# A mixture-of-experts loop in 64-row matmul pairs, with a ring of four results that GpSimd copies

## What is computed

```python
ggates, gidx = _topk_gates(xf @ Wg + bg, 2)                  # 2 of 4 groups
egates, eidx = _topk_gates(einsum('nd,gde->nge', xf, We) + be, 4)   # 4 of 8 experts in each
combine = gw[:, :, None] * ew                                # weight of each token and expert
for g in range(4):
    h = gelu(einsum('nd,edm->enm', xf, W1[g]) + b1[g][:, None, :])  # 192 -> 768
    o = einsum('enm,emd->end', h, W2[g]) + b2[g][:, None, :]        # 768 -> 192
    y = y + einsum('end,ne->nd', o, combine[:, g, :])
```

## Time and profile before

| | us |
|---|---|
| median of three runs | 752.56 |
| the three runs | 750.7, 752.56, 757.16 |
| the profiled execution | 756.36 |
| its span, first to last instruction | 754.6 |
| TensorE busy in the span | 679.0 |
| GpSimd busy in the span | 304.8 |
| VectorE busy in the span | 406.5 |
| ScalarE busy in the span | 239.0 |

### The profile page before, as it was taken

How to read it: one execution, slowest core, us unless ns; L and a number is a source line. 1 busy time by engine, 2 the same in 40 slices (tenths; PEclk the granted TensorE clock), 3 DMA queues, 4 the chain that set the end, 5 groups by cost and what they waited for, 6 DMA issues and landing times.

```text
span 754.6 us, 20437 instructions
## 1 busy us (share of the span) xinstructions
PE 679.0 (90%) x6550; PEld 574.3 (76%) x6550; DVE 406.5 (54%) x1222; ACT 239.0 (32%) x686; POOL 304.8 (40%) x288
## 2 busy tenths in 40 slices
PE   6986948898989999876899799999999999999994
PEld 4754735655755797753799699999999999999994
DVE  6645572845489688878544234444444444444442
ACT  3322312123238311115143233333333333333331
POOL 0111820011023636302354455555655555656554
PEclk9996959587999999975699899999999999999998
DMA  9910000000000003041258454465546566565422
GB/s 325 266 41 2 2 3 2 3 1 3 1 1 0 2 1 120 8 162 50 52 151 234 113 140 127 121 171 113 129 106 178 147 172 171 117 173 126 97 46 39
DMA packets 36136, 70.07 MB, mean 93 GB/s; under 512 B 6481, under 2 KB 21362, under 8 KB 36082
## 3 DMA queue, kind: packets, MB, share of 16 engines
q0 software_dynamic: 15840, 17.71, 13.9%
q10 hardware_dynamic: 8064, 33.12, 12.8%
q1 hardware_dynamic: 12178, 18.48, 7.9%
HBM read 59.31 MB, written 9.98 MB: 92 GB/s over the span
## 4 chain that ended last, share of the span: by engine, by line
PE 72%; DVE 17%; issue 4%; DMA 3%; ACT 1%; POOL 1%; DVEq 0%; ACTq 0%; POOLq 0%; SPq 0%
PE bank L1617 20%; PE bank L1609 14%; PE bank L1612 9%; PE bank L1435 4%; PE bank L1589 4%; PE bank L1367 4%; PE bank L1299 3%; DMA out_dram<-arena,number_u 2%; PE bank L1387 2%; DVE stats L941 1%; DVE zx L955 1%; PE bank L1378 1%; DVE arena L1175 1%; DVE arena L1172 1%; PE bank L1405 1%
## 5 line engine op out<-in xcount | busy, mean ns | idle before, releaser
L654 POOL DMA_INDIRECT out_dram<-arena,number_u x80 | 126.8, 1585 | 54.9 <-DMA out_dram<-arena,number_u 28.1
L648 POOL DMA_INDIRECT arena<-normed_rows,fetch_u x80 | 78.4, 980 | 113.8 <-DMA out_dram<-arena,number_u 42.1
L841 ACT ACTIVATE arena<-bank,arena 128x128 f32<-128x128 f32 x234 | 64.6, 375 | 120.9 <-PE bank L1612 116.9
L1260 DVE COPY arena<-bank 128x256 f32<-128x256 f32 x81 | 34.4, 425 | 118.4 <-PE bank L1589 109.8
L1617 PE MATMUL bank<-arena 128*128 128x192 f32 x468 | 83.4, 327 | 0.7 <-ACT arena L841 0.7
L1617 PEld LDWEIGHTS bank<-arena 128*128 128x128 f32 x468 | 76.0, 191 | 1.0 <-ACT arena L841 1.0
L1279 DVE TENSOR_SCALAR arena<-bank,arena 128x192 f32 x80 | 33.4, 418 | 62.2 <-PE bank L1617 60.6
L1609 PE MATMUL bank<-arena 128*128 128x128 f32 x468 | 60.1, 279 | 4.3 <-DVE arena L1260 4.3
L1609 PEld LDWEIGHTS bank<-arena 128*128 128x128 f32 x468 | 58.3, 195 | 5.1 <-DVE arena L1260 5.1
L551 POOL TENSOR_SCALAR rstd<-mv 128x4 f32<-128x4 f32 (+1 forms) x15 | 3.6, 237 | 143.5 <-DVE mv L944 143.5
L841 ACT ACTIVATE arena<-bank,w_space 128x128 f32<-128x128 f32 x132 | 36.4, 375 | 68.6 <-PE bank L1612 68.6
(11 more groups left out here) (259 smaller groups left out, 1235.0 us busy)
## 6 DMA issues: line engine op xcount, KB each, us to landing
arena<-in_moe_w_dram ACTq DMA_DIRECT2D x14, 579.0 KB, 5.7
arena<-in_moe_w_dram ACTq DMA_DIRECT2D x14, 576.0 KB, 4.3
arena<-in_xf_dram SPq DMA_DIRECT2D x16, 256.0 KB, 10.6
w_space<-in_moe_w_dram ACTq DMA_DIRECT2D x7, 579.0 KB, 5.4
w2small<-in_moe_w_dram ACTq DMA_DIRECT2D x7, 579.0 KB, 5.7
w_space<-in_moe_w_dram ACTq DMA_DIRECT2D x7, 576.0 KB, 3.8
wab<-in_moe_w_dram ACTq DMA_DIRECT2D x7, 576.0 KB, 4.1
arena<-in_w_dram SPq DMA_DIRECT2D x8, 480.0 KB, 7.4
```

The source lines that it names most:

```text
L648: pool.indirect_dma_start(out=mo_stage[:, s * ROWN:(s + 1) * ROWN], out_offset=None, in_=normed_rows, in_offset=bass.IndirectOffsetOnAxis( ...
L654: pool.indirect_dma_start(out=out, out_offset=bass.IndirectOffsetOnAxis(ap=number_u[:, s:s + 1], axis=0), in_=mo_res[:, s * D:(s + 1) * D] ...
L841: nc.scalar.activation(mo_hT[:, m, :], bank[2 + m][:, 0:P], ACT.Gelu, bias=b1[:, m:m + 1]).then_inc(free[2 + m], 1)
L1260: nc.vector.tensor_copy(mo_xT.rearrange("p k t -> p (k t)"), bank[1][:, 0:2 * P]).then_inc(free[1], 1)
```

## The change

Both layers and the transposes run on 64 rows. The weights of the first layer are laid out so that each half of the partitions holds three of the six chunks; the rows of a tile are staged twice, once for each half, and their transposes come out in both halves of the array, behind the first layer's results in banks 2 and 5. A tile makes 9 pairs for the first layer, 3 pairs of transposes and 6 pairs for the second layer, whose halves go to banks 0 and 1 and are added by VectorE. TensorE waits for the rows to transpose ahead of the last pair of the first layer. VectorE writes its scaled result into a ring of four; GpSimd copies it from there to `mo_res`, copies the row numbers too, and waits for its copy before the store. VectorE's 32 experts are written out, with the bounds loaded one expert ahead.

```diff
+CHUNKS = D // 64
+HIDDEN_DONE = tuple(m + half for m in range(MC // 2) for half in (0, MC // 2))
+COLUMNS_AT, COLUMN_BANKS = P, (2, 2 + MC // 2)
+RESULTS = 4
-W1N = HID + MC // 2 * P
+W1N = MC // 2 * CHUNKS * P
...
-                use(5, "table", 1)
+                use(7, "table", 1)
...
+            pool.sem_inc(sem("result_free"), RESULTS)
             with pool.Fori(0, pairs) as pair:
...
+                    tile, new = pool.snap(i + 0), pool.snap(i % RESULTS * D)
                     pool.wait_ge(sem(f"accumulated{s}"), added)
-                    pool.sem_inc(sem("result_free"), 1)
+                    nc.gpsimd.tensor_copy(number_u[:, s:s + 1], table_u[:, bass.ds(tile, 1)])
                     pool.wait_ge(sem("fetch_set"), fetch_set)
...
                     pool.wait_ge(sem("result_ready"), result)
+                    pool.sem_inc(sem("adding"), 1)
+                    nc.gpsimd.tensor_copy(mo_res[:, s * D:(s + 1) * D], mo_new[:, bass.ds(new, D)]).then_inc(sem("result_free"), 1)
+                    pool.wait_ge(sem("result_free"), pool.snap(i + (RESULTS + 1)))
                     pool.sem_inc(sem("adding"), 1)
                     pool.wait_ge(sem(f"accumulated{1 - s}"), settled)
...
-                    act.wait_ge(full[0], i + moe_base[0])
-                    for m in range(MC):
+                    act.wait_ge(full[1], i + moe_base[1])
+                    for m in HIDDEN_DONE:
...
             def stage_rows(i):
                 dve.wait_ge(sem("rows_in"), i * 16 + 16)
-                dve.wait_ge(full[1], i + moe_base[1])
+                if not isinstance(i, int) or i:
+                    dve.wait_ge(sem("columns_full"), i)
                 nc.vector.tensor_copy(mo_gates[:, bass.ds(i % 4 * NE, NE)], mo_stage[:, bass.ds(i % STAGE * ROWN + D, NE)])
-                nc.vector.tensor_copy(mo_x[:, D:2 * P], mo_stage[:, bass.ds(i % STAGE * ROWN + P, REST)])
-                nc.vector.tensor_copy(mo_x[:, 0:D], mo_stage[:, bass.ds(i % STAGE * ROWN, D)]).then_inc(sem("rows_staged"), 1)
+                for half in range(2):
+                    ins = nc.vector.tensor_copy(mo_x.rearrange("p (k h x) -> p k h x", k=CHUNKS, h=2)[:, :, half, :], mo_stage[:, bass.ds(i % STAGE * ROWN, D)].rearrange("p (k x) -> p k x", k=CHUNKS))
+                ins.then_inc(sem("rows_staged"), 1)
 
             def take_columns(i):
-                dve.wait_ge(full[1], i + (moe_base[1] + 1))
-                nc.vector.tensor_copy(mo_xT.rearrange("p k t -> p (k t)"), bank[1][:, 0:2 * P]).then_inc(free[1], 1)
+                dve.wait_ge(sem("columns_full"), i + 1)
+                for r, b in zip((0, REST), COLUMN_BANKS):
+                    ins = nc.vector.tensor_copy(mo_xT[:, :, r:r + REST], bank[b][:, COLUMNS_AT:COLUMNS_AT + D].rearrange("p (k t) -> p k t", k=CHUNKS))
+                ins.then_inc(sem("columns_taken"), 1)
...
-                    dve.wait_ge(full[0], summing)
-                    ts(out=mo_new[:, bass.ds(new, D)], in0=bank[0][:, 0:D], scalar1=mo_gates[:, bass.ds(gate, 1)], scalar2=None, op0=ALU.mult).then_inc(free[0], 1)
-                    dve.sem_inc(sem("scaling"), 1)
                     dve.wait_ge(sem("result_free"), added)
                     dve.sem_inc(sem("scaling"), 1)
-                    nc.vector.tensor_copy(number_u[:, bass.ds(half, 1)], table_u[:, bass.ds(tile, 1)])
-                    dve.wait_ge(free[0], summing)
-                    nc.vector.tensor_copy(mo_res[:, bass.ds(to, D)], mo_new[:, bass.ds(new, D)]).then_inc(sem("result_ready"), 1)
+                    dve.wait_ge(full[0], low)
+                    ts(out=mo_new[:, bass.ds(new, D)], in0=bank[0][:, 0:D], scalar1=mo_gates[:, bass.ds(gate, 1)], scalar2=None, op0=ALU.mult).then_inc(free[0], 1)
+                    dve.wait_ge(full[1], high)
+                    dve.wait_ge(free[0], low)
+                    stt(out=mo_new[:, bass.ds(new, D)], in0=bank[1][:, 0:D], scalar=mo_gates[:, bass.ds(gate, 1)], in1=mo_new[:, bass.ds(new, D)], op0=ALU.mult, op1=ALU.add).then_inc(free[1], 1)
+                    dve.wait_ge(free[1], high)
+                    dve.sem_inc(sem("result_ready"), 1)
+
+            first, end = expert_start(dve, 0, 0), expert_start(dve, 1, 1)
+            for e in range(NE):
+                after = expert_start(dve, e + 2, 1) if e + 2 <= NE else None
+                weighted_tiles(e, first, end)
+                first, end = end, after
...
+            def transpose_rows():
+                for k in range(CHUNKS):
+                    at = COLUMNS_AT + k * REST
+                    for r, b in zip((0, REST), COLUMN_BANKS):
+                        ins = nc.tensor.transpose(bank[b][:, at:at + REST], mo_x[r:r + REST, k * P:(k + 1) * P], ident[r:r + REST, r:r + REST])
+                ins.then_inc(sem("columns_full"), 1)
...
-                    pe.wait_ge(free[1], i + (moe_base[1] + 1))
-                    for m in range(MC):
-                        mm(bank[2 + m][:, 0:P], w1e[:, m * P:(m + 1) * P], mo_xT[:, 0, :], start=True, stop=False)
-                    for m in range(MC):
-                        r, c = m % 2 * REST, HID + m // 2 * P
-                        mm(bank[2 + m][:, 0:P], w1e[r:r + REST, c:c + P], mo_xT[r:r + REST, 1, :], start=False, stop=True).then_inc(full[2 + m], 1)
-                    transpose_rows(i + 1)
+                    pe.wait_ge(sem("columns_taken"), i + 1)
+                    for n in range(MC // 2):
+                        for k in range(CHUNKS):
+                            c = (n * CHUNKS + k) * P
+                            if n * CHUNKS + k == MC // 2 * CHUNKS - 1:
+                                pe.wait_ge(sem("rows_staged"), i + 2)
+                                for b in COLUMN_BANKS:
+                                    pe.wait_ge(free[b], i + (moe_base[b] + 1))
+                            for r, m in ((0, n), (REST, n + MC // 2)):
+                                ins = mm(bank[2 + m][:, 0:P], w1e[r:r + REST, c:c + P], mo_xT[r:r + REST, k, :], start=(k == 0), stop=(k == CHUNKS - 1))
+                                if k == CHUNKS - 1:
+                                    ins.then_inc(full[2 + m], 1)
+                    transpose_rows()
                     pe.wait_ge(free[0], i + moe_base[0])
-                    for m in range(MC):
+                    pe.wait_ge(free[1], i + moe_base[1])
+                    for n, m in enumerate(HIDDEN_DONE):
                         pe.wait_ge(free[2 + m], i + (moe_base[2 + m] + 1))
-                        ins = mm(bank[0][:, 0:D], mo_hT[:, m, :], w2e[:, m, :], start=(m == 0), stop=(m == MC - 1))
-                    ins.then_inc(full[0], 1)
+                        for r, b in ((0, 0), (REST, 1)):
+                            ins = mm(bank[b][:, 0:D], mo_hT[r:r + REST, m, :], w2e[r:r + REST, m, :], start=(n == 0), stop=(n == MC - 1))
+                            if n == MC - 1:
+                                ins.then_inc(full[b], 1)
```

More of the change, by code:

```diff
@@ L291, in vit_tower @@
         mo_gates = view(P, 4 * NE)
-        mo_x = view(P, 2 * P)
-        mo_xT = view(P, 2 * P).rearrange("p (k t) -> p k t", k=2)
+        mo_x = view(P, CHUNKS * P)
+        mo_xT = view(P, CHUNKS * P).rearrange("p (k t) -> p k t", k=CHUNKS)
         mo_res = view(P, 2 * D)
-        mo_new = view(P, 4 * D)
+        mo_new = view(P, RESULTS * D)
         mo_w1 = [w1_space[:, 0:W1N], wab[:, 0:W1N]] + [view(P, W1N) for _ in range(2)]
@@ L831, in expert @@
                 if e and e + AHEAD - 1 < NE:
-                    act.wait_ge(full[0], first + moe_base[0])
+                    act.wait_ge(full[1], first + moe_base[1])
                     load_expert(act, (u + AHEAD - 1) % AHEAD, e + AHEAD - 1)
@@ L1266, in _, with weighted_tiles @@
             stage_rows(1)
-            with dve.Fori(0, NE) as e:
-                first = dve.value_load(starts[0:1, bass.ds(e, 1)], min_val=0, max_val=MAXT - 1)
-                end = dve.value_load(starts[0:1, bass.ds(e + 1, 1)], min_val=1, max_val=MAXT)
+            def weighted_tiles(e, first, end):
                 with dve.Fori(first, end) as i:
@@ L1272, in _ @@
                     stage_rows(i + 2)
-                    gate, to = dve.snap(i % 4 * NE + e), dve.snap(i % 2 * D)
-                    new = dve.snap(i % 4 * D)
-                    added, summing = dve.snap(i + 1), dve.snap(i + (moe_base[0] + 1))
-                    half, tile, ahead = dve.snap(i % 2), dve.snap(i + 0), dve.snap(i + 4)
+                    gate, new = dve.snap(i % 4 * NE + e), dve.snap(i % RESULTS * D)
+                    added, low, high = dve.snap(i + 1), dve.snap(i + (moe_base[0] + 1)), dve.snap(i + (moe_base[1] + 1))
+                    half, ahead = dve.snap(i % 2), dve.snap(i + 4)
                     nc.vector.tensor_copy(fetch_u[:, bass.ds(half, 1)], table_u[:, bass.ds(ahead, 1)]).then_inc(sem("fetch_set"), 1)
-                    dve.wait_ge(full[0], summing)
```

(20 more changed lines are left out.)

3 lines of the change are left out of this document (1 added, 2 removed).

## The result

The changed kernel takes 779.39 us in the median (776.01 to 788.1), the kernel before 752.11: a ratio of 1.0345, with a 95% interval from 1.0288 to 1.0401. One of its four runs, that of 788.1 us, was in a slower state and is left out of the ratio; the median of the other three is 777.07. The profiled execution took 776.01 us, its span 774.2; that is 19.7 more than the profiled execution of before, and the loop holds nearly all of it.

The account below looks back on a forecast made before the run. TensorE sets the pace at 4.53 us a tile, with GpSimd as late. GpSimd's loop grows 28.5 us to 395.3, less half of 5: +26 on the profiled 756.36 gives 782, less 3.8 to the median, 778; range 738 to 798.

Parts of the forecast that it names:

- the mechanism that it named: GpSimd's loop: two added copies and a wait lengthen undisturbed fetch spacing, so late landings are not made up; +26 us.
- The distance: GpSimd's loop: undisturbed time from one fetch start to the next grows from 3.50 to 4.37 us.
- The long distances: GpSimd's loop: 28 fetch spacings stretched by landings late behind expert loads, together 172.4 us, were to stay.
- The step to the median: Whole run: 3.8 us subtracted from 782, as the profiled execution before lay that far above its median; 778.
- TensorE's tile: TensorE, one tile of 128 rows: 4.53 us becomes 4.35, 0.18 saved, 14 us in all.
- The wait ahead of the last first-layer pair: TensorE waits for staged rows and GELUs: hidden by 0.2 us; uncovered, 0.1 to 0.2 in each of 28 loading tiles.
- VectorE's slack: VectorE's loop: some 0.5 us more a tile, 3.2 in all, hidden under 4.35; dropped bounds loads come from the same slack.
- Hidden: Rival, GpSimd: store made ready during the copy, fetch spacing near 3.50, 14 to 16 us gone, 737 us; chance 0.18.
- Cancelled: Rival: fetch spacing of 3.8 us leaves GpSimd's loop at 366 as before, 752 us; chance 0.12.
- Collision: Rival: each GpSimd copy waits out a VectorE copy of 0.26 us, spacing 4.63, 791 us; chance 0.10.
- No overlap at 192 columns: Rival, TensorE's second layer: pairs run one after the other, 1.96 us more a tile, about 910 us; chance 0.03.
- What would show it: Signs: chain leaves TensorE, spacing near 4.4, 0.9 us idle before store, TensorE stopped, last store over 2.5 us behind last matmul.

Follow-up runs that it names:

- run 2: Kernel before with only the ring of four, GpSimd copying results and row numbers, without 64-row pairs or written-out experts: 788.3 us, ratio 1.0514.
- run 1: Changed kernel with VectorE again copying row numbers and results; 64-row pairs and written-out experts stay: 750.24 us, ratio 0.9987.
- run 3: Changed kernel with GpSimd's copy of the result moved ahead of its fetch, the wait for it left ahead of the store: 758.28 us, ratio 1.0056.
- run 8: Changed kernel with VectorE's experts in a loop again, both bounds loaded at each expert's begin: 793.01 us, ratio 1.0526.
- run 4: Changed kernel with GpSimd's copy of the result made twice, first into a spare buffer: 799.3 us, ratio 1.0645.
- run 7: Run 1's kernel with one landing semaphore per stage, so a fetch no longer waits for the landing of the fetch before: 744.11 us, ratio 0.9865.
- run 11: Run 1's kernel with VectorE's experts in a loop again, so the 64-row pairs and earlier transposes alone: 753.32 us, ratio 0.9991.
- run 12: Changed kernel with VectorE's experts in a loop and without the loads of experts 4 to 31 (edits of runs 8 and 5): 742.41 us, ratio 0.9845.
- run 5: Changed kernel without the loads of experts 4 to 31, the four held experts serving in turn: 738.87 us, ratio 0.9812.

## Why the prediction was right

The forecast of 778 us and its sign hold, by the mechanism that it named. That the forecast is within 2 us is luck: steps that were off made up for one another. The ring costs 3 to 5%, alone (run 2) and within the change (run 1 against it); the pairs alone cost and give nothing. Its steps, one by one:

- **The distance** came to 4.40 in the median, where the sum was 4.37. The copy took 0.36 (predicted 0.33), the wait behind it 0.94 or 1.06 (0.93), number copy and gap 0.36 up to the next fetch (0.45 with both gaps), fetch and store 0.03 more each. Run 3, which takes the wait for the copy out of the line, leaves a distance of 4.05 in the median and not 3.6, since TensorE's tile or the landing of a store then sets many of the turns.
- **The long distances** were mis-sized. I let 28 stand with 172.4 us; 23 with 139.6 are left, and five more short ones (over 5 us the kernel before has 30 with 182.8; I had left out two near the end). That is the 9.6 us by which the loop is shorter than the 395.3 forecast. The longer plain distance does not explain it: run 8 has the same one, and 30 long ones with 190.9 us, a loop of 404.6. What differs is the wait of stores for the landing of the store before, which I had not priced by itself: counted as in run 3, it is 12.8 us in the kernel before, 17 to 22 in runs 2, 3, 4 and 8, and only 2.7 here. That the changed kernel all but escapes it is the luck in the forecast. What I read of late fetches stands: in the earlier trace rows the view names a store's landing ahead of 570.25, but by the trace's record the fetch before had landed at 569.45, 0.80 us ahead.
- **The step to the median** hid this: I subtracted 3.8 us because the profiled execution of before lay above its median, while that of after lies 3.4 below its own (1.1 below 777.07). Profiled execution against profiled execution I said 782, and it was 776.
- **TensorE's tile** was 4.35 and is 4.20. The term that failed is the transposes: 0.18 for three pairs, near the low end of 0.16, where I had taken 0.34 because no step in the rows was shorter than 0.11. A pair of 64 columns does take about half the time of one of 128. As said there, the forecast did not rest on it.
- **The wait ahead of the last first-layer pair** is hidden in plain tiles, as said. In loading tiles I had 0.1 to 0.2; tiles of 4.5 show 0.3. With GpSimd setting the pace it should cost the changed kernel nothing, which no run tests; in run 7 it is seen.
- **VectorE's slack** held in its words and failed in its result. I costed the dropped loads of bounds at nothing, since VectorE has slack for them. Without the ring that is so (runs 1 and 11), and with the ring and no expert loads the loop costs some 3.5 us (run 12 against 5). But in the changed kernel the written-out experts are worth 13.6 (run 8), in stores' landings that I had not priced at all. Without that gain the median would have been 793, still inside the range.
- **The rivals.** *Hidden* (737) needed a store made ready under the copy: 0.94 of idle time is there. *Cancelled* (752) needed a distance of 3.8. *Collision* (791) needed 4.63 and longer GpSimd work; the copy has 0.36, and the fetches, at 1004 ns against 979 before, have 25 ns more and no wait of 0.26; the 45 fetches that run beside a copy of rows on VectorE (L1266) take 1004 ns in the median, the other 35 take 1005. The rule of the Trainium skill on the shared ports (SBUF — State Buffer, section Who interferes with whom) is not borne out as a cost here. *No overlap at 192 columns*: the second layer's 24 passes take 2.01 us in pairs, where one after the other they would take 24 x 0.163 = 3.9.
- **What would show it.** The chain left TensorE, the idle time stands between copy and store, TensorE is stopped for staged rows at the end of its first layer (L1636 behind L1266). The last store's generation ends at 768.83 and the last matmul began its second layer at 757.10: it is far more than the 2.5 us said.

```profile
757.10 2.20 PE L1645 MATMUL bank<-arena 64*128 64x192 f32 x24
```

```profile
767.22 1.61 POOL L663 DMA_INDIRECT out_dram<-arena,number_u  x1 [1.06 <-DMA out_dram<-arena,number_u]
```

That is 768.83 - 759.30 = 9.5 us: TensorE ends two tiles ahead of GpSimd, whose line runs on at 4.3 to 4.4.

## What to carry to other kernels

An engine that is busy for half of the time can still set the pace, if its work for a tile is a line of waits: before work is moved to it, add up its line with the waits, set it against the pace of the others, and put what it copies where a transfer is in flight (run 3: one moved line, 21 us). Where a serial line waits for landings, an edit elsewhere that shifts it against large loads can be worth 14 us though its own stall is hidden: test such edits in the version that they go into. The name that a profile gives to the end of a wait is the event that came last; before building on it, see whether the kernel asks for that event there, and whether the idle time changes with the name. A faster TensorE shows only when rows land in time: shorter pairs and one landing semaphore per stage each gave nothing alone, and with the experts written out beside them 1.4%.

## What the runs showed of the hardware

- A gather's landing depends on what else is in flight. In the changed kernel 48 fetches land 1.71 us behind the end of their generation on average and 32 land 3.72 behind it; without expert loads (run 5) 74 of 79 distances are plain.
- An indirect DMA on GpSimd starts 0.30 us behind another one, but 0.94 (in odd turns 1.06) behind a copy whose end it waits for, and 0.8 behind a landing that it waits for.
- On 64 rows an fp32 pass of a pair takes 2.01/36 = 0.056 us at 128 columns, 2.01/24 = 0.084 at 192, and 0.18/6 = 0.03 for the 64-column transposes.
